# Where the attention's transposes land in PSUM: four banks instead of three, and one full-width transpose for the relative sums

## The reference, cut to what matters

```python
rel_pos = arange(L)[None, :] - arange(L)[:, None] + (MAX_LEN - 1)   # clamped/wrapped by indexing
rel_k, rel_v = relative_k[rel_pos], relative_v[rel_pos]              # (L, L, 8)
scores = einsum('bhld,bhrd->bhlr', Q, K) * scale + einsum('bhld,lrd->bhlr', Q, rel_k)
attn = softmax(scores, axis=-1)
out = einsum('bhlr,bhrd->bhld', attn, V) + einsum('bhlr,lrd->bhld', attn, rel_v)
x = x + (out.transpose(0, 2, 1, 3).reshape(B, L, D) @ Wo.T + bo)
x = x + ffn(layernorm(x))     # shared experts + two of eight experts
```

## Time and profile before

| | us |
|---|---|
| median of 3 runs | 2294.86 |
| lowest, highest | 2294.36, 2295.84 |
| the profiled execution | 2293.6 |
| its span, first to last instruction | 2291.8 |
| PE busy | 2193.1 (96%) |
| DVE busy | 1700.9 (74%) |
| ACT busy | 1540.5 (67%) |
| POOL busy | 1058.9 (46%) |
| granted TensorE clock, mean | 0.989 |

### The profile page before, as it was taken

One profiled execution on the slowest core, in us unless ns is written; L12 is line 12 of the kernel. 1 busy time (PEld: TensorE's weight loads), 2 busy tenths in 40 slices (PEclk: granted clock), 3 DMA queues, 4 the chain that ended last, 5 costly groups with the idle time before them and its releaser, 6 DMA issues.

```text
span 2291.8 us, 90552 instructions
## 1 busy us (share of the span) xinstructions
PE 2193.1 (96%) x37570; PEld 1533.2 (67%) x37570; DVE 1700.9 (74%) x3703; ACT 1540.5 (67%) x3290; POOL 1058.9 (46%) x991
## 2 busy tenths in 40 slices
PE   3999999999989999999899999999998999999998
PEld 2666666666666666666666666666666777777776
DVE  4777787778777877778677878787775667666665
ACT  3666666666665666666566666666665888888886
POOL 2444344334333433343344344333431777776776
PEclk7999999999999999999999999999998999999999
DMA  4112211321221122112211311222111221222120
GB/s 131 33 50 62 69 51 42 81 59 43 63 70 42 51 62 69 51 42 67 65 52 41 81 51 51 62 60 60 42 51 41 25 27 18 27 23 27 23 23 11
DMA packets 249555, 114.67 MB, mean 50 GB/s; under 512 B 140170, under 2 KB 245012, under 8 KB 249204
## 3 DMA queue, kind: packets, MB, share of 16 engines
q1 hardware_dynamic: 249204, 109.59, 19.6%
HBM read 83.34 MB, written 8.39 MB: 40 GB/s over the span
## 4 chain that ended last, share of the span: by engine, by line
PE 76%; DVE 7%; ACT 6%; issue 5%; POOL 3%; SPq 1%; DMA 0%; DVEq 0%; ACTq 0%; POOLq 0%
PE ps L1221 18%; PE ps L1238 11%; PE ps L1169 10%; PE ps L1176 8%; PE ps L1248 6%; PE ps L1187 6%; DVE neg_max L778 3%; POOL probs_t L489 3%; ACT probs L635 2%; ACT probs L568 2%; PE ps L1262 2%; PE ps L1409 2%; PE ps L1392 2%; PE ps L1394 2%; PE ps L1393 2%
## 5 line engine op out<-in xcount | busy, mean ns | idle before, releaser
L568 ACT ACTIVATE probs<-ps,neg_max 128x512 f32<-128x512 f32 x1024 | 694.4, 683 | 474.3 <-DVE neg_max L778 474.3
L778 DVE TENSOR_REDUCE neg_max<-ps 128x1 f32<-128x512 f32 (+1 forms) x768 | 619.5, 862 | 190.0 <-PE ps L1176 190.0
L428 POOL TENSOR_TENSOR stat_hi<-q_twice,mask8h 128x1024 f16<-128x1024 f16 x128 | 243.2, 1900 | 944.1 <-PE ps L1176 835.4
L1221 PE MATMUL ps<-const,probs 128*128 128x128 f32 x4096 | 548.5, 280 | 30.4 <-DVE probs_t L784 12.4
L1221 PEld LDWEIGHTS ps<-const,probs 128*128 128x128 f32 x4096 | 446.6, 142 | 132.4 <-issue 45.3
L784 DVE COPY probs_t<-ps 128x512 f32<-128x512 f32 x512 | 339.9, 684 | 159.7 <-PE ps L1221 157.1
L557 ACT ACTIVATE probs_t<-ps 128x512 f32<-128x512 f32 x512 | 297.9, 597 | 141.6 <-PE ps L1221 140.5
L489 POOL TENSOR_TENSOR probs_t<-probs,probs_t 128x1024 f16<-128x1024 f32 x160 | 340.0, 2133 | 108.8 <-ACT probs_t L641 108.8
L1169 PE MATMUL ps<-keys,stat_hi 128*32 128x512 f16 x4096 | 317.3, 385 | 0.6 <-issue 0.6
L1176 PE MATMUL ps<-rk_split,stat_rel 96*32 96x512 f16 (+1 forms) x4096 | 285.9, 354 | 0.0
L988 DVE SCALAR_TENSOR_TENSOR keys<-ps,comb,keys 128x128 f32<-128x128 f32 x640 | 179.8, 344 | 129.4 <-PE ps L1411 129.4
(11 more groups left out here) (135 smaller groups left out, 2781.1 us busy)
## 6 DMA issues: line engine op xcount, KB each, us to landing
rv_step<-in_rv_win SPq DMA_DIRECT2D x128, 512.0 KB, 3.8
keys<-keys SPq DMA_DIRECT2D x64, 96.0 KB, 2.6
x_pair<-in_x SPq DMA_DIRECT2D x8, 512.0 KB, 4.5
q_twice<-q_hi SPq DMA_DIRECT2D x32, 128.0 KB, 2.8
q_lo_pair<-q_lo SPq DMA_DIRECT2D x32, 128.0 KB, 2.6
rel_scratch<-rel_t SPq DMA_DIRECT2D x128, 32.0 KB, 3.5
x_pair<-in_x SPq DMA_DIRECT2D x16, 256.0 KB, 3.3
x_pair<-rel_scratch SPq DMA_DIRECT2D x64, 64.0 KB, 3.9
```

Of the source, the lines that this page charges most:

```text
L568: nc.scalar.activation(probs[:, q, :], ps[:, i, :], ACT.Exp, bias=neg_max[:, q:q + 1], accum_out=row_sum[parity][:, s * QUADS + q:s * QUAD ...
L778: nc.vector.tensor_reduce(neg_max[:, IN_ROUND * j + at:IN_ROUND * j + at + n], ps[:, at:at + n, :], op=ALU.max, axis=AX_X, negate=True).th ...
L1221: last = nc.tensor.transpose(ps[:, TR_BANK + (q + 1) % TR_BANKS, rt * P:(rt + 1) * P], probs[:, q, rt * P:(rt + 1) * P], ident)
```

## The change: what it does

A round's transposes get the banks `(0, 4, 5, 6)`: quad 0 goes into bank 0 once that round's first exponential has read it, the other three have a bank each. In the rounds with relative queries, which use banks 0 and 1, quad 0 goes into bank 6, and quad 3, which has it too, waits for quad 0's evacuation. Before the next scores, PE now also waits until quad 0 has been evacuated. Pieces move to bank 1.

`rel_o` is padded to 128 columns (the new half zeroed once by POOL), so one 128x128 transpose replaces two of 32 columns. It goes to columns 256 to 383 of bank 7, behind the value products and the piece, right before the round's transposes; DVE copies 64 x 128 instead of 32 x 256, after the sums of the values instead of before. `relative_products` of the next step wait for that copy, and the store is two DMAs of 32 partitions by 128 columns.

```diff
-TR_BANK, TR_BANKS = 4, 3
+TR_BANKS = (0, 4, 5, 6)
+PIECE_BANK = 1
...
+def tr_bank(q, piece):
+    return TR_BANKS[3 if piece and piece.startswith("relative") and q % IN_ROUND == 0 else q % IN_ROUND]
...
-        rel_o = sb("rel_o", [P, 2, 32])
-        rel_t = sb("rel_t", [32, 2, 2 * P])
+        rel_o = sb("rel_o", [P, 4, 32])
+        rel_t = sb("rel_t", [64, 2, P])
...
-                sp.dma_start(rel_scratch[bass.ds(row, 32), s * 2 * P:(s + 1) * 2 * P], rel_t[:, s % 2, :]).then_inc(rel_stored[s % 2], 16)
+                for half in range(2):
+                    cols = slice((2 * s + half) * P, (2 * s + half + 1) * P)
+                    sp.dma_start(rel_scratch[bass.ds(row, 32), cols], rel_t[32 * half:32 * half + 32, s % 2, :]).then_inc(rel_stored[s % 2], 16)
...
+            nc.gpsimd.memset(rel_o[:], 0.0).then_inc(setup_pool, 1)
...
-                nc.vector.tensor_copy(rel_t[:, s % 2, :], ps[0:32, TR_BANK, 0:2 * P]).then_inc(rel_t_ready, 1)
+                nc.vector.tensor_copy(rel_t[:, s % 2, :], ps[0:64, AV_BANK, 2 * P:3 * P]).then_inc(rel_t_ready, 1)
...
                     if products:
+                        reduce_values(*trailing)
                         rel_out(*trailing)
-                        reduce_values(*trailing)
-                    evacuate(pair, s, 0)
-                    evacuate(pair, s, 1)
+                    evacuate(pair, s, 0, piece)
+                    evacuate(pair, s, 1, piece)
...
                 round_read(pair, s, j, IN_ROUND)
 
+                if j == 1:
+                    evacuated(pair, s, 0)
+                elif s:
+                    evacuated(pair, s - 1, IN_ROUND)
+                elif not first:
+                    evacuated(pair - 1, STEPS - 1, IN_ROUND)
...
                 for q in range(IN_ROUND * j, IN_ROUND * (j + 1)):
-
-                    if q >= TR_BANKS:
-                        evacuated(pair, s, q - TR_BANKS)
-                    elif q == 2 and (s >= 2 or not first):
-                        pe.wait_ge(rel_t_ready, START + pair * STEPS + s - 1)
-                    elif s:
-                        evacuated(pair, s - 1, (6, 7, 5)[q])
-                    elif not first:
-                        evacuated(pair - 1, STEPS - 1, (6, 7, 5)[q])
+                    bank = tr_bank(q, piece)
+                    if bank == TR_BANKS[0]:
+                        if here:
+
+                            round_read(*here[0:3], 1)
+                        else:
+                            evacuated(pair, s, 0)
+                    else:
+
+                        last_q = TR_BANKS.index(bank)
+                        if q % IN_ROUND == 3 and tr_bank(0, piece) == bank:
+                            evacuated(pair, s, IN_ROUND * j)
+                        elif j:
+                            evacuated(pair, s, last_q)
+                        elif s:
+                            evacuated(pair, s - 1, IN_ROUND + last_q)
+                        elif not first:
+                            evacuated(pair - 1, STEPS - 1, IN_ROUND + last_q)
...
                 if half == 0:
+
+                    pe.wait_ge(rel_t_ready, START + pair * STEPS + s)
                     pe.wait_ge(rv_landed, START + (pair * STEPS + s + 1) * 16)
...
-            def rel_transposes(pair, s, after):
+            def rel_transposes(pair, s):
 
                 pe.wait_ge(rel_reduced, START + pair * STEPS + s + 1)
-
-                if after:
-                    evacuated(*after, 5)
-                else:
-                    pe.wait_ge(rel_t_ready, START + pair * STEPS + s)
-                for half in range(2):
-                    last = nc.tensor.transpose(ps[0:32, TR_BANK, half * P:(half + 1) * P], rel_o[:, half, :], ident)
-                last.then_inc(rel_tr, 1)
+                nc.tensor.transpose(ps[:, AV_BANK, 2 * P:3 * P], rel_o[:].rearrange("p a r -> p (a r)"), ident).then_inc(rel_tr, 1)
```

More of the change, by code:

```diff
@@ L233, in attention_ffn @@
         SETUP_DVE = 10
-        SETUP_POOL = 3
+        SETUP_POOL = 4
         STAT_OPS = 4
@@ L598, in last_step @@
                 s = STEPS - 1
-                evacuate(pair, s, 1)
+                evacuate(pair, s, 1, None)
                 normalised(0, 0)
@@ L822, in score_round @@
                     if piece == f"values{b}":
-                        values(pair, b, 0)
+                        values(pair, b, PIECE_BANK)
                     if piece == f"relative{b}":
@@ L832, in score_round @@
                     if transposed:
-                        evacuate(*before, IN_ROUND)
+                        evacuate(*before, IN_ROUND, piece)
                     if products:
@@ L836, in score_round @@
                     if transposed:
-                        evacuate(*before, IN_ROUND + 1)
+                        evacuate(*before, IN_ROUND + 1, piece)
                     if products:
@@ L1103, in piece_read, with next_scores_wait @@
                     pe.wait_ge(operands_ready, START + pair * 6 + 6)
-            def next_scores_wait(pair, s, j, ahead):
+            def next_scores_wait(pair, s, j, first, ahead):
                 if (s, j) == (STEPS - 1, ROUNDS - 1) and not ahead:
@@ L1203, in evacuated, with transposes @@
                 pe.wait_ge(evac_dve if q % IN_ROUND < 2 else evac_act, START + done)
-            def transposes(pair, s, j, first, after=None):
+            def transposes(pair, s, j, first, piece, here=None):
                 pe.wait_ge(exp_done, START + pair * TILES + s * QUADS + IN_ROUND * (j + 1))
                 for q in range(IN_ROUND * j, IN_ROUND * (j + 1)):
-                    if q >= TR_BANKS:
-                        evacuated(pair, s, q - TR_BANKS)
-                    elif q == 2 and (s >= 2 or not first):
-                        pe.wait_ge(rel_t_ready, START + pair * STEPS + s - 1)
-                    elif s:
-                        evacuated(pair, s - 1, (6, 7, 5)[q])
-                    elif not first:
-                        evacuated(pair - 1, STEPS - 1, (6, 7, 5)[q])
+                    bank = tr_bank(q, piece)
[14 more added lines that the diff above has]
+                            evacuated(pair - 1, STEPS - 1, IN_ROUND + last_q)
                     for rt in range(RT):
-                        if after and (q % IN_ROUND, rt) == (IN_ROUND - 1, RT - 1):
-                            next_scores_wait(*after)
-                        last = nc.tensor.transpose(ps[:, TR_BANK + (q + 1) % TR_BANKS, rt * P:(rt + 1) * P], probs[:, q, rt * P:(rt + 1) * P], ident)
+                        if here and (q % IN_ROUND, rt) == (IN_ROUND - 1, RT - 1):
+                            next_scores_wait(*here)
+                        last = nc.tensor.transpose(ps[:, bank, rt * P:(rt + 1) * P], probs[:, q, rt * P:(rt + 1) * P], ident)
                     last.then_inc(tr_done, 1)
@@ L1272, in score_round @@
                 else:
-                    if s >= 2:
-                        rel_transposes(pair, s - 2, (pair, s - 1))
-                    elif s and not first:
-                        rel_transposes(pair - 1, STEPS - 1, (pair, 0))
-                    elif not first:
-                        rel_transposes(pair - 1, STEPS - 2, (pair - 1, STEPS - 1))
                     for b in range(2):
```

71 lines of the change are left out of this document (38 added, 33 removed).

## The result

The changed kernel takes 2238.25 us (median of 4 runs, 2234.7 to 2239.29); the kernel before, beside it, 2295.23 (4 runs, 2294.36 to 2295.84). The ratio is 0.975 with a 95% interval of 0.973 to 0.977: 57.0 us faster, where 73.9 were forecast. The range of 2207 to 2240 held the time, near its upper end; the estimate was 17 us too low, and the time is 5 us outside the 2209 to 2233 that the forecast gave itself at 0.81. The profiled execution took 2237.4, its span is 2235.6.

What follows compares the result with a forecast made beforehand. PE was taken as the bound (busy 96% of the span). Gains of 49.0 + 6.5 + 4.2 + 2.7 + 8.9 + 2.6 = 73.9 us took 2294.9 to 2221.0; range 2207 to 2240.

Steps and rivals of the forecast that it cites:

- rival B: DVE takes the bound: late relative copy delays quad 0's evacuation, 0.15 us per second round, 2240 us; chance 0.07.
- Relative sums: One full tile behind the products replaces two narrow transposes: 0.355 us gained per second round where nothing else binds.
- The 0.46: Cost in us of the two narrow transposes, 4.61 - 4.15, in each of 126 second rounds.
- pitch of 0.105: Spacing in us of neighbouring 128x128 transposes' loads, taken as the full relative tile's cost on PE.
- Rival A: Full tile costs more than a pitch: own drain of 0.20 us, 2246 us, or all 0.46, 2266; chance 0.08.
- the 0.20 ahead of the full-width transposes: Gap in us between products and transposes, read as a tiling-mode drain, paid once in both orders.
- Quad 3's hole of 0.15: Among a round's transposes, quad 3 waits for quad 0's bank to be emptied; new banks gain 0.15 us.
- It doesn't bind: Last transpose's new wait for quad 0's evacuation: done at T + 1.44 against T + 1.575, 0.13 us to spare.
- First rounds of late steps: First rounds gain 0.14 us in steps 8 and 14, some 0.06 in steps 11 and 13.
- 0.06 of DVE's backlog: In step 13's second round, added to exponentials' end and 0.30: 6.60 us for 6.69, 0.09 gained.
- Second rounds of steps 11 and 13: Step 11 as a plain round gains 0.50 us; step 13 turns exponential-bound and gains 0.09.
- rivals C and D: C: late relative copy ages quad 0 and maxima, about 2309 us, chance 0.02. D: clock loss, given no term.

Runs made afterwards that it cites:

- e6: Changed kernel with the old banks (quads in 4 to 6, pieces in bank 0, no wait for quad 0 before the next scores): 2254.88 us, ratio 0.982.
- e7: Changed kernel with the full-width relative transpose between scores and products, in bank 4, its copy ahead of the sums of values: 2268.18 us, ratio 0.988.
- e4: Changed kernel with two 128x32 relative transposes again, but behind the products in bank 7; DVE copies 32x256: 2248.21 us, ratio 0.980.
- e1: Changed kernel with the wait for quad 0's evacuation put ahead of the wait for the exponentials: 2239.24 us, ratio 0.976.
- e8: e2 plus e1's wait order only in first rounds of steps 2 to 7 of pairs inside the hardware loop: 2220.69 us, ratio 0.968.
- e2: Changed kernel with GpSimd's spread of relative queries held in some steps until DVE's preparation operation of that round is done: 2222.43 us, ratio 0.969.
- e10b: Changed kernel with the same kind of wait on GpSimd in steps 5, 6, 8, 11, 13, without such DVE operations: 2237.86 us, ratio 0.975.
- e9b: e8 with DVE's second split of queries moved from round (13,0) to the end of round (14,1): 2219.95 us, ratio 0.968.

## Why the prediction was right or wrong, by its steps

*The range: held by luck.* Its upper end, 2240, was the price of rival B, a relative copy that comes too late in each second round. That did not happen. What brought the time to 2238 was a term that neither the forecast nor any rival had priced, in the first rounds, so the range held for no reason of its own.

*Relative sums: right in size, half right in reason.* 0.355 was forecast, 0.35 measured (e6 alone). The 0.46 was read as what "the two narrow transposes cost". They cost 0.06 to 0.07 more than a full one; 0.28 to 0.29 was their place, with a gap of 0.42 behind the scores. Had the full tile stayed in the old place (e7), the forecast's pitch of 0.105 would have been wrong by that much. The 0.105 itself stands: 0.11 measured. Rival A, a gap of its own for the full tile, did not happen in the new place and did in the old one. The forecast took the 0.20 ahead of the full-width transposes as the sign of a change of tile mode; e4 has it ahead of narrow ones, so the width alone does not make it.

*Banks: right, but for the new wait.* Quad 3's hole of 0.15 measured 0.13 (6.29 in e6, 6.16 after): right in second rounds, but in the first rounds the banks brought the loss of the next paragraph with them. The wait for quad 0's evacuation has nothing to hold in plain second rounds, since the 16 loads stand without a hole: rival B did not occur there. It binds where the forecast had it bind, in the rounds that project values; 0.93 forecast, 0.91 measured. The copy of the sums took 0.28 for 0.26 and ended at T + 0.68 counted from the first probabilities' load (800.19 - 799.51) for T + 0.54, 0.06 before quad 0's evacuation starts, a smaller cover than was worked out and still enough.

*The new wait, costed at nothing: wrong.* "It doesn't bind" was true and not the question. Behind the exponentials' wait it costs 0.08 or 0.09 in each looped round in which the exponentials end last: 24 rounds of steps 2 to 5, 2.0 us, and the 0.08 forecast as gained in 12 rounds of steps 6 and 7, 0.9 us. The runs e1 and e8 show it by undoing it, e6 by not having the wait. Why a fulfilled wait costs this in the loop and not in pairs 0 and 7, and why those two lost 0.06 a round with the other order, is open.

*First rounds of late steps: the step that failed.* The forecast gave steps 8, 11, 13 and 14 a gain of 0.06 to 0.14, with "0.06 of DVE's backlog" for a DVE that is late. It took port operations as of fixed length. They are not: beside GpSimd's spread they end at a fixed distance behind it (0.55 the subtractions, 0.28 the cast, 0.08 the normalising operation), and GpSimd is tied to scores, so DVE's lead over the old kernel was lost there and the maxima came 0.5 later, counted from a round start that had moved forward. e2 shows it by undoing it, e10b is its control. In this sense the general part of rival B, DVE as the bound, came true, but in other rounds and not through the relative copy. This is 10.5 us in the seven pairs that prepare a next one (measured against forecast, steps 8, 11, 13, 14) and 0.6 in the last pair's step 9. With the 2.9 of the wait and a single round, pair 5's first, that was 1.9 longer than forecast in this execution, it makes the 15.8 (the others cancel) between +11.5 and -4.3, which is near what the hold of e2 is worth by chance only, since that hold gains more in some rounds than was lost there. The 2.0 of the last phase is not explained; over the profiled executions of all runs that phase takes 550.7 to 553.6. The sign stood in the timeline behind the earlier trace rows: the next operation of DVE takes 1.84 us (above) for a 128x512 from SBUF, where the evacuation of as many elements takes 0.68, and that was not asked about. The groups of DVE by line would have shown a mean of 1227 ns, and the line's instances 0.75 and 1.84 us by turns.

*Second rounds of steps 11 and 13.* 0.50 and 0.09 were forecast, 0.25 and 0.44 measured; the errors cancel, and with them the sum of second rounds (62.5 for 62.4) looks better than its terms. Step 13 was taken as exponential-bound by the times of before; after the change part of DVE's delay had gone to the round ahead of it (e2 gives it back: 6.73). Step 11 was not looked into.

*Stores, padding, clock: right.* Nothing of them is seen, nor of rivals C and D. The 256 stores of 16 KB land in 3.2 us for 3.5 before, and the granted clock was 1.00 in the window of the attention phase above, with 17 transposes in a row in each second round.

## What to carry to other kernels

When an edit lets TensorE start earlier, list what does not start earlier with it: here an operation on GpSimd, and the DVE operations that share its access to SBUF. A DVE duration that differs between two instances of one shape was here a wait, though the profile counts it as busy; look at both instances before costing it as work. A cheap hold on GpSimd until such an operation is done brought 14 to 15.8 us, and the best version, e8 or e9b, stands at 2220 to 2221 us, 0.968 of the kernel before.

## What the runs showed of the hardware that was not expected

- DVE's subtractions with two SBUF inputs take 0.69 to 0.74 us alone and 1.78 to 2.20 when they start during GpSimd's 96x1024 multiplication, and end 0.55 after it; the cast from SBUF to SBUF 0.42 and 1.04 to 1.40, ending 0.28 after; the normalising operation, 128x128 in SBUF, 0.34 and 1.38 to 1.71, ending 0.08 after. Evacuations from PSUM (0.68), maxima from PSUM and the sums of values, a reduction in SBUF (0.27 and 0.28), take the same with GpSimd beside them or without.
- A fulfilled wait behind one for the exponentials costs 0.08 us on PE in looped pairs and nothing in unrolled ones. With the two waits the other way round (e1) the looped pairs gain the 0.08 back in these rounds, lose as much in others, and the unrolled pairs lose 0.06.
- A full-width transpose costs 0.39 us between scores and 32-column products, 0.11 next to other full-width transposes; two 32-column ones cost 0.46 and 0.17.
